# Gated decay attention: the values of two groups projected together, as three products of rounded parts

## The reference, cut to what matters

```python
q = (hidden_states @ Wq.T).reshape(B, L, H, D)
k = (hidden_states @ Wk.T).reshape(B, L, KVH, D)
v = (hidden_states @ Wv.T).reshape(B, L, KVH, D)      # <- the values
q, k = _apply_rope(q, cos, sin), _apply_rope(k, cos, sin)
...
y_intra = einsum('bhnij,bhnjd->bhnid', scores * decay, xc)   # xc = v * dt
...
y = y / rms * gnorm_w
gate = (hidden_states @ Wg.T).reshape(B, L, H, D)
y = y * (gate * sigmoid(gate))
return y.reshape(B, L, H * D) @ Wo.T
```

## Time and profile before

| | us |
|---|---|
| median of three runs | 1466.83 |
| the profiled execution, its own time | 1464.51 |
| its span, first to last instruction | 1462.1 |
| TensorE busy | 1410.8 (96% of the span) |
| VectorE / ScalarE / GpSimd busy | 1093.5 / 857.0 / 604.8 |
| mean granted TensorE clock | 0.989 of full speed |

### The profile page before, as it was taken

How to read it: one execution, slowest core, us unless ns; L and a number is a source line. 1 busy time by engine, 2 the same in 40 slices (tenths; PEclk the granted TensorE clock), 3 DMA queues, 4 the chain that set the end, 5 groups by cost and what they waited for, 6 DMA issues and landing times.

```text
span 1462.1 us, 24367 instructions
## 1 busy us (share of the span) xinstructions
PE 1410.8 (96%) x7654; PEld 1177.7 (81%) x7654; DVE 1093.5 (75%) x2492; ACT 857.0 (59%) x2152; POOL 604.8 (41%) x631
## 2 busy tenths in 40 slices
PE   8999999999989989999999999879999999999997
PEld 7888888887778867787778778668888888888875
DVE  5697666787687977766776776768788788887885
ACT  4656555655223157656755755638677677677661
POOL 3555444434022137556655745334243242242221
PEclk9999999999999999999999999999999999999999
DMA  8011110112122241330321231310012022012000
GB/s 323 1 73 73 73 72 9 63 33 102 58 87 92 109 145 45 113 118 30 130 101 54 104 101 58 130 73 30 17 72 87 15 73 86 15 72 78 1 0 29
DMA packets 30133, 107.72 MB, mean 74 GB/s; under 512 B 3847, under 2 KB 13191, under 8 KB 22104
## 3 DMA queue, kind: packets, MB, share of 16 engines
q1 hardware_dynamic: 30040, 106.58, 20.0%
HBM read 97.07 MB, written 9.50 MB: 73 GB/s over the span
## 4 chain that ended last, share of the span: by engine, by line
PE 56%; DVE 18%; issue 13%; POOL 7%; ACT 5%; POOLq 0%; DMA 0%; DVEq 0%; ACTq 0%; SPq 0%
PE bank L186 11%; PE bank L187 11%; PE bank L188 11%; PE bank L1808 3%; POOL yss L1438 2%; PE bank L318 2%; PE bank L1823 2%; PE bank L341 2%; PE bank L1829 2%; PE bank L1825 2%; PE bank L287 2%; DVE logit L2120 1%; POOL tmp L159 1%; PE bank L1262 1%; PE bank L1766 1%
## 5 line engine op out<-in xcount | busy, mean ns | idle before, releaser
L159 POOL TENSOR_TENSOR tmp<-tmp,sin 128x512 f32<-128x512 f32 x80 | 112.0, 1399 | 221.5 <-ACT tmp L152 221.5
L188 PE MATMUL bank<-wo_low,att_high 128*128 128x512 f32 x384 | 150.8, 393 | 0.0
L2120 DVE SCALAR_TENSOR_TENSOR logit<-bank,qss,amask 128x512 f32<-128x512 f32 x128 | 90.9, 747 | 57.1 <-PE bank L188 55.9
L2026 POOL TENSOR_TENSOR qss<-qss,half 128x4 f32<-128x4 f32 x32 | 34.9, 1090 | 199.6 <-DVE qss L2106 199.6
L1638 PE MATMUL bank<-kT,wg 128*128 128x256 f32 x512 | 113.1, 383 | 4.2 <-ACT prob L1672 4.2
L1927 ACT ACTIVATE prob<-logit,rmax 128x512 f32<-128x512 f32 x128 | 91.6, 719 | 37.8 <-DVE rmax L2124 37.8
L1638 PEld LDWEIGHTS bank<-kT,wg 128*128 128x128 f32 x512 | 98.1, 192 | 18.1 <-ACT prob L1672 4.6
L186 PE MATMUL bank<-l_wo_high,att_high 128*128 128x512 f32 x256 | 105.0, 410 | 1.8 <-DVE att_low L1522 1.1
L187 PE MATMUL bank<-xT_high,wq_low 128*128 128x512 f32 x256 | 102.3, 400 | 0.0
L187 PE MATMUL bank<-l_wo_high,att_low 128*128 128x512 f32 x256 | 100.0, 391 | 0.0
L1941 ACT ACTIVATE p_high<-bank 128x512 fp32r<-128x512 f32 x128 | 70.0, 596 | 45.1 <-PE bank L1808 44.8
(11 more groups left out here) (290 smaller groups left out, 4443.4 us busy)
## 6 DMA issues: line engine op xcount, KB each, us to landing
wq<-in_l_wq SPq DMA_DIRECT2D x16, 1024.0 KB, 6.9
wo<-in_l_wo SPq DMA_DIRECT2D x16, 1024.0 KB, 4.9
wkv<-in_l_wkv SPq DMA_DIRECT2D x16, 512.0 KB, 5.6
wg<-in_l_wg SPq DMA_DIRECT2D x8, 1024.0 KB, 4.8
wq<-in_x_wq SPq DMA_DIRECT2D x8, 1024.0 KB, 7.1
wo<-in_x_wo SPq DMA_DIRECT2D x8, 1024.0 KB, 4.9
kT<-in_x_wkv SPq DMA_DIRECT2D x8, 512.0 KB, 4.1
kv_keys<-logit SPq DMA_DIRECT2D x8, 512.0 KB, 4.6
```

Of the source, the lines that this page charges most:

```text
L159: eng.tensor_tensor(halves(tmp[4 + j % 2]), halves(tmp[2 + j % 2]), per_batch(sin), ALU.mult).then_inc(sem(f"{l}_sinp"), 1)
L188: return eng.matmul(dst, a_high, b_low, start=False, stop=stop)
L2120: dve.scalar_tensor_tensor(logit[s % 2][:, c, :], bank[3 + c][:, :], qss[p][:, 1, h, 2 * b + c:2 * b + c + 1], amask[:, c, :], ALU.mult, A ...
```

## The change

- The raw weights are laid out anew: the key weight of a group comes alone (`l1_wk`, 256 KB, to `l1_key_raw` on the place of wkv[1]); the value weights of two groups come as one 256-column tile (`l1_wv`, 512 KB, to wkv[0]).
- Groups 0 and 1: `first_values` projects both ahead of group 0, still directly in f32, with 256 columns in each matmul.
- Groups 2 to 7: the pair of groups g+2, g+3 (g even) is projected in groups g and g+1: in each body two row tiles, t = 2p (slot 0) and t = 2p + 1 (slot 1), in three matmuls of rounded parts with 256 columns, over four chunks. The places on TensorE are those of the slots before. Groups 6 and 7 project no values.
- The high part of the pair's weight is made by ScalarE in even groups after sigmoid(1), ahead of the next query weight (`high_values`, two copies of 128x512); the low part by GpSimd in even groups, after gated(1) and ahead of the next query weight's low part (two subtractions of 128x512, in place).
- ScalarE copies the values out with two instructions in even groups and three in odd groups, before with one.
- The loads of a pair's value weight stand in SyncE's order before the loads ahead of the odd group.

`value` goes, with its calls. `tail` is true in groups 6 and 7.

```diff
+        def first_values():
+            pe.wait_ge(sem("l1_wv"), 16)
+            for t in range(NT):
+                for c in range(KC):
+                    last = pe.matmul(bank[4 + t // 2 * 2][:, t % 2 * L:(t % 2 + 1) * L], xT[:, c, t * P:(t + 1) * P],
+                                     wkv[0][:, c, :], start=(c == 0), stop=(c == KC - 1))
+            last.then_inc(sem("l1_kvdone"), 1)
...
+                def values(slot):
+                    t = 2 * p + slot
+                    if slot == 0:
+                        if p == 0:
+                            pe.wait_ge(sem("l1_vlow"), g + 2)
+                        pe.wait_ge(sem("l1_gclamp"), 4 * n)
+                    for c in range(KC):
+                        last = product(pe, bank[0][:, slot * L:(slot + 1) * L],
+                                       [part[c][:, t * P:(t + 1) * P] for part in l1_xT],
+                                       [part[:, c, :] for part in l1_wv], c == 0, c == KC - 1)
+                    if slot:
+                        last.then_inc(sem("l1_kvdone"), 1)
...
                 if not last_group:
                     key(n, bank[1])
-                    value(n, 1 - p, (0, 1), bank[0])
+                if not tail:
+                    values(0)
                 outputs(1, 0)
...
-                if not last_group:
-                    value(n, 1 - p, (2, 3), bank[0])
+                if not tail:
+                    values(1)
...
+                def high_values():
+                    act.wait_ge(sem("l1_wv"), 8 * g + 32)
+                    for c in range(0, KC, 2):
+                        act.activation(l1_wv[0][:, c:c + 2, :], wkv[0][:, c:c + 2, :], ACT.Copy)\
+                           .then_inc(sem("l1_vhigh"), 1)
...
                 sigmoid(1)
+                if p == 0 and not tail:
+                    high_values()
                 if not last_group:
                     act.wait_ge(sem("l1_wq0"), 16 * (g + 2))
                     high_weights(act, l1_wq_high, wq[0])
...
                 gated(0)
                 gated(1)
+                if p == 0 and not (isinstance(g, int) and g >= NG - 2):
+                    for c in range(0, KC, 2):
+                        pool.wait_ge(sem("l1_vhigh"), g + 1 + c // 2)
+                        pool.tensor_tensor(l1_wv[1][:, c:c + 2, :], wkv[0][:, c:c + 2, :],
+                                           l1_wv[0][:, c:c + 2, :].bitcast(F32), ALU.subtract)\
+                            .then_inc(sem("l1_vlow"), 1)
                 if not last_group:
                     pool.wait_ge(sem("high_part"), l1_wo_high_at(g) + 1)
                     low_weights(pool, "split", l1_wq_high, wq_low[0], wq[0])
...
-            with nc.sync.Fori(1, NG // 2) as i:
-                for p in range(2):
-                    l1_load_ahead(sp, 2 * i + p, p)
+            with nc.sync.Fori(1, NG // 2 - 1) as i:
+                l1_load_ahead(sp, 2 * i, 0)
+                l1_load_values(sp, i + 1)
+                l1_load_ahead(sp, 2 * i + 1, 1)
+            for g in range(NG - 2, NG):
+                l1_load_ahead(sp, g, g % 2)
```

More of the change, by code:

```diff
@@ L1062, in decoder_kernel @@
                  [over(f"l1_xT_low{c}", [P, T], host, T * 4)[:, :] for c, host in enumerate(("kT0", "kT1", "v0", "v1"))])
+        l1_key_raw = nc.alloc_sbuf_tensor_at("l1_key_raw", [P, KC, HD], F32, offset=address["wkv1"])
+        l1_v_kept = nc.alloc_sbuf_tensor_at("l1_v_kept", [P, 2, HD], F32, offset=address["wkv1"] + KC * HD * 4)
+        l1_wv = [over(f"l1_wv_{part}", [P, KC, 2 * HD], host) for part, host in (("high", "klow0"), ("low", "wkv0"))]
         l1_wk = [over(f"l1_wk{i}", [P, KC, HD], "amask", i * C * 4) for i in range(2)]
@@ L1165, in weights_of, with l1_load_keys, l1_load_values @@
             return a[name][bass.ds(g, 1)].rearrange("a p c n -> (a p) c n")
[L1167 to L1170, removed]
+        def l1_load_keys(sp, g):
+            if due(g):
+                sp.wait_ge(sem("split"), L0_SPLIT + 4 * (g - 1) + 2)
+            sp.dma_start(l1_key_raw[:, :, :], weights_of("l1_wk", g)).then_inc(sem("l1_wk"), 16)
+        def l1_load_values(sp, m):
+            if due(m):
+                sp.wait_ge(sem("l1_kvdone"), 2 * m - 1)
+            sp.dma_start(wkv[0][:, :, :], weights_of("l1_wv", m)).then_inc(sem("l1_wv"), 16)
         def l1_load_queries(sp, g):
@@ L1187, in l1_load_ahead @@
         def l1_load_ahead(sp, g, p):
-            l1_load_keys(sp, g, p)
+            l1_load_keys(sp, g)
             l1_load_rows(sp, g, p)
@@ L1207, in key @@
                 project_split(pe, dst[:, :], l1_wk, slice(0, HD), l1_xT, "l1_proj")
[L1209 to L1214, removed]
+            def first_values():
+                pe.wait_ge(sem("l1_wv"), 16)
+                for t in range(NT):
                     for c in range(KC):
[L1216 to L1219, removed]
+                        last = pe.matmul(bank[4 + t // 2 * 2][:, t % 2 * L:(t % 2 + 1) * L], xT[:, c, t * P:(t + 1) * P],
+                                         wkv[0][:, c, :], start=(c == 0), stop=(c == KC - 1))
+                last.then_inc(sem("l1_kvdone"), 1)
             def body(g, p, last_group):
+                tail = isinstance(g, int) and g >= NG - 2
                 n = g + 1
                 g_first = isinstance(g, int) and g == 0
+                def values(slot):
[10 more added lines that the diff above has]
+                        last.then_inc(sem("l1_kvdone"), 1)
                 def query(h):
@@ L1320, in body @@
                 turn_z(3)
-                if not last_group:
-                    value(n, 1 - p, (2, 3), bank[0])
+                if not tail:
+                    values(1)
                 out_tile(2)
                 out_tile(3)
-            value(0, 0, (0, 1, 2, 3), bank[4])
+            first_values()
             pe.wait_ge(sem("low_part"), L1_LOW + KC)
@@ L1331, in l1_scalar, with pair, first_values, values @@
         def l1_scalar(act):
[L1332 to L1337, removed]
-            def body(g, p, last_group):
+            def pair(t):
+                return t[:, :].rearrange("p (t n d) -> p t n d", t=2, n=2)
+            def first_values():
+                act.wait_ge(sem("l1_kvdone"), 1)
+                for half_ in range(2):
+                    for n in range(2):
+                        last = act.activation(v[n][:, 2 * half_:2 * half_ + 2, :], pair(bank[4 + 2 * half_])[:, :, n, :],
+                                              ACT.Copy)
+                last.then_inc(sem("l1_v"), 1)
+            def body(g, p, last_group):
+                tail = isinstance(g, int) and g >= NG - 2
+                def values():
+                    act.wait_ge(sem("l1_kvdone"), g + 2)
+                    act.wait_ge(sem("l1_y"), 4 * (g + 1))
+                    act.activation(v[0][:, 2 * p:2 * p + 2, :], pair(bank[0])[:, :, 0, :], ACT.Copy)
+                    if p == 0:
+                        last = act.activation(l1_v_kept[:, :, :], pair(bank[0])[:, :, 1, :], ACT.Copy)
+                    else:
+                        act.activation(v[1][:, 2:4, :], pair(bank[0])[:, :, 1, :], ACT.Copy)
+                        last = act.activation(v[1][:, 0:2, :], l1_v_kept[:, :, :], ACT.Copy)
+                    last.then_inc(sem("l1_v"), 1)
+                def high_values():
[3 more added lines that the diff above has]
+                           .then_inc(sem("l1_vhigh"), 1)
                 def decays(b):
@@ L1408, in body @@
                 headed(3)
-                if not last_group:
-                    value(n, 1 - p, bank[0])
+                if not tail:
+                    values()
             rope_psum_copies(act, "l1", 0, 0, bank[3])
-            value(0, 0, bank[4])
+            first_values()
             act.wait_ge(sem("dt"), 2)
@@ L1419, in l1_gpsimd_first @@
         def l1_gpsimd_first(pool):
-            l1_split_keys(pool, 0, 0)
+            l1_split_keys(pool, 0)
             pool.wait_ge(sem("high_part"), L1_HIGH + 1)
@@ L2324, in _ @@
             l1_load_queries(sp, 0)
-            l1_load_keys(sp, 0, 0)
+            l1_load_keys(sp, 0)
+            l1_load_values(sp, 0)
             sp.dma_start(wg[0][:, :, :], a["ctxT"][0]).then_inc(sem("ld_ctxT0"), 16)
@@ L2476, in key_value, with value_pairs @@
         return np.concatenate([by_group(wk), by_group(wv)], axis=3)
+    def value_pairs(w):
+        return np.concatenate([by_group(w)[0::2], by_group(w)[1::2]], axis=3)
     def out_by_group(w):
@@ L2518 @@
         "l1_wq": by_group(g["L1_attn_Wq"]),
-        "l1_wkv": key_value(g["L1_attn_Wk"], g["L1_attn_Wv"]),
+        "l1_wk": by_group(g["L1_attn_Wk"]),
+        "l1_wv": value_pairs(g["L1_attn_Wv"]),
         "l1_wo": out_by_group(g["L1_attn_Wo"]),
```

12 lines of the change are left out of this document (6 added, 6 removed).

## The result

The changed kernel takes 1470.46 us, the median of 21 runs (1466.21 to 1472.33), beside 1466.34 us for the kernel before in as many (1461.23 to 1470.68). The ratio is 1.0028, 95% interval 1.0019 to 1.0037: slower by 4.1 us (2.8 to 5.4). The forecast was 7 us slower. The ratios in this document leave out two executions that ran far slower than all others (2013 us at a granted clock of 0.652, and 3160 us).

A forecast was written before the change was run, and what follows sets the result against it. Two equally long chains, TensorE's own work and GpSimd's through wq_low and power, were taken to bound each group's middle. The terms +3.7 + 4.4 - 1.8 - 0.95 + 1.7 = +7.05 gave 1473.9 us; 8-in-10 range 1466.0 to 1479.5.

The forecast's parts named there:

- The bound: Mid-group, TensorE's own chain and GpSimd's through wq_low and power are equally long; z(1) has no room.
- Slot 0 worth 0: TensorE's first value slot, ahead of outputs(1,0), saves 0.4 us, worth 0 because TensorE then waits for z(1).
- Slot 1: TensorE's second value slot, ahead of out_tile(2), shrinks from 1.70 to 1.4 us: -0.3 in each of six groups, -1.8.
- Group 6: It loses both value slots; of slot 1's 1.7 us, out_tile(2) takes back its wait for att_low: -0.95 us.
- GpSimd in groups 2 and 4: Two added subtractions between gated(1) and wq_low delay power(0), and so z, by 2.2 us a group; +4.4 together.
- The upper bound: Each of VectorE's four subtractions stops GpSimd once, at the full 0.6 us: +3.3 in place of +2.2.
- Start and group 0: Longer first_values and GpSimd's six subtractions make power(0) of group 0 late: +3.7 us, between 2.8 and 4.4.
- The clock: TensorE's waits for z in even groups halve its clock in one group of three: +1.7 us, possible 0 to 5.7.
- Rival B: The clock falls in all three even groups and turns cost fully: +13.2, 1480 us; milder mix 1477.5; chance 0.22.
- Two signs named in advance: TensorE waits over 1 us for z twice per even group; granted clock under 1 in even groups' second half.
- the rivals: Six outcomes for the total time, the forecast itself included, with chances 0.45, 0.22, 0.15, 0.09, 0.09 and 0.01.

The follow-up runs named there:

- The two added subtractions: The kernel before with two more GpSimd subtractions of 128x512 between gated(1) and wq_low in groups 0, 2 and 4: 1473.27 us, ratio 1.0046.
- the order with wq_low last: Powers and means moved early, wq_low behind power(3): on top of both moves 1456.18 us, ratio 0.9932; in the kernel before 1462.51 us, ratio 0.9974.
- the two fills: The kernel before with two GpSimd constant fills between gated(1) and wq_low in groups 0, 2 and 4: 1466.26 us, ratio 1.0002.
- both orders of the powers in the kernel before: The kernel before with powers and means moved early: wq_low behind power(1), 1477.16 us, ratio 1.0080; wq_low behind power(3), 1462.51 us, ratio 0.9974.
- the powers first on top of both moves: On top of both moves, power(0) and power(1) ahead of wq_low, and VectorE's mean(0) and mean(1) earlier: 1475.41 us, ratio 1.0064.
- both moves: Changed kernel, value weight's high part before sigmoid(0), low part between gated(0) and gated(1), dt_turn ahead of group 0's query(1): 1463.84 us, ratio 0.9977.

## Why the prediction was right, and where not

- **The bound.** Right. That z(1) had no room was read from 0.14 to 0.17 us between its end and TensorE's start. The two added subtractions in the kernel before, and the order with wq_low last, show it from both sides: 2.5 us of GpSimd cost 2.25 a group, and slot 0's saving counts only where z is early. One thing was left out: VectorE's mean, too, came just behind wq_low, and power(0) waited 0.28 for it, so three roads of about equal length met and not two.
- **Slot 0 worth 0.** Right: it is the wait of 0.33 in odd groups. **Slot 1**, -0.3 a group: measured -0.33 to -0.38 in groups 1, 3, 5 and 6 of the table.
- **Group 6**, -0.95: measured 52.29 - 51.35 = 0.94 in the step to group 7.
- **GpSimd in groups 2 and 4**, +2.2 between 1.6 and 3.3: measured 1.92 and 1.98 in the period, 2.25 and 2.31 with slot 1's 0.33 put back. The six subtractions took 8.93, forecast 8.9, with three turns as counted: VectorE's four took 0.68, 1.77, 1.76 and 1.78. The Trainium skill says that a GpSimd operation shuts out a VectorE operation with two SBUF inputs if it reads SBUF itself, and not if it only writes ("SBUF — State Buffer", section "SBUF: two separate sides"); the trace agrees, since GpSimd's fills leave wo_low at 4.65 and its subtractions make it 5.75. The upper bound, a turn with each of VectorE's four, was not reached here: VectorE's first subtraction started before gated(1), at 667.59 against 667.99.
- **Start and group 0**, +3.7 between 2.8 and 4.4: outputs(1,1) of group 0 came 4.0 us later in the first pair of profiles and 5.0 in the second, outside the bounds; without what had arisen ahead of 518 us it is 3.7 and 3.6. That this fits so well is partly luck. dt_turn was late by 2.1 and not 3.3. The fall of the clock behind query(2) was counted as the same before and after; it lasted from 538 to 542 us before and from 540 to 547 after, which costs about as much as the fall at 518 that the changed kernel did not have. GpSimd's start was late by 1.75 (gated(1) ended at 561.99 against 560.24), not by the estimated 1.0, and its six subtractions took 8.93 in the first profile and 9.34 in the second, where all four of VectorE's were stopped (6.79 in place of 4.65), as the forecast of 9.4 had it.
- **The clock**, +1.7 for one fall of three: this step failed. After waits of 1.7 and 0.76 with 1.6 of work between, the granted clock stayed at 1.00 in groups 2 and 4 of both profiles, and in group 0. Rival B, with three falls, is out. Group 2, first profile:

```profile
676.00:690.00 14.00, 11.56 (x73) 10.05 (x72) 8.68 (x23) 9.17 (x28) 9.37 (x9) 1.00 0.17 71
```

- Two signs named in advance did not come: the second wait of an even group is 0.76 and not over 1, and the granted clock is not under 1 there. The chances of the rivals add up to 1.01.

The terms without the clock are 3.7 + 4.4 - 1.8 - 0.95 = +5.35, and the profiles show 5.2 and 5.1 from 518 us to group 7. The medians differ by 4.1 only, and the granted clock that is on record for each execution explains part of the rest. A line fitted through 33 executions of the changed kernel and 108 of the kernel before, on several chips, gives 0.7 us for each thousandth of granted clock, and at equal clock a difference of 4.6 us (4.3 to 5.0); at 0.989, for example, the means are 1468.1 (11 executions) and 1464.4 (16). The changed kernel's clock is on average a little higher (0.9876 against 0.9870), which gives 0.4 us back. So over the whole program the clock was worth about -0.4 in place of the forecast +1.7: the total lay in the range, but 1.7 of the 7 us forecast were for a fall that never came. About 0.5 us between 5.1 and 4.6 stays open.

What lies behind group 7 took 517.3 to 522.2 us in the profiles, in kernels that are the same there, with the clock at half in other places each time. The kernel before had some 6 us at half clock in group 7 in one profile (3 us lost) and none in the other; both profiles of the changed kernel had falls near 984 and 1001 us that neither profile of the kernel before had.

## What to carry to other kernels

TensorE at 96% busy does not mean that what it saves is time: look at the few hundredths between the end of what it waits for and its start, since two roads of equal length show almost no wait. Work added to an engine that is 41% busy cost more than the saving it served, because of where it stood; the same work in a gap of 2.7 us, where that engine waited anyway, was free, and taking the long item (wq_low, 5.8 us, needed 20 us later) off that road, together with the means on VectorE, took off more than the change had added. Before moving work into a gap, ask what it stands in front of next: the powers and means put first, with wq_low behind them, made the kernel before 12 us slower (ratio 1.0080).

## What was not expected of the hardware

The same wait of 3.2 us in the same kernel was followed by some 6 us at half clock in one execution and by none in another. Waits of 1.68 and 0.76 us around 1.6 us of matmuls left the clock at full in the even groups of both profiles of the changed kernel. Waits of 1.20 and 0.83 around 1.1 us were followed by half clock in the two profiles of the kernel before. Waits of 1.23 to 1.44 and 0.83 were not, in the profiles of four runs whose TensorE program is the same up to there (the two subtractions, the two fills, and both orders of the powers in the kernel before), nor were 1.21 and 0.83 in the first profile of the changed kernel: the stretch from 518 to 520 us reads 0.50 in the one case and 1.00 in the other. With the powers first on top of both moves, a wait of 1.67 at the turn of z(3) was followed by some 3 us at half clock in groups 0 and 4, which is why the columns g1 and g5 read 55.7, and not in the other groups. So a fall that was seen once behind a wait is a chance and not a price, and one profile does not show how large the chance is.

A tiny operation can be held by a long one of another engine: VectorE's mean of 128x4 took 1.32 us in place of 0.15 where it started beside a subtraction of GpSimd.
